# Sums of products in sixteen 32x32 tiles over four PSUM banks, block reads packed by parity, and one written-out order

## The reference, cut to what matters

```
a = k_l[..., :, None] * v_l[..., None, :]
out = einsum('bhs,bhst->bht', r_l, faaaa * a + s)
s = a + w_l[..., None] * s
```

## Time and profile before

| | us |
|---|---|
| three timed runs, median (lowest to highest) | 872.42 (869.52 to 874.44) |
| span of the profiled execution, first to last instruction | 871.9 |
| PE busy in it | 813.5 (93%) |
| DVE busy | 602.6 (69%) |
| ACT busy | 354.4 (41%) |
| POOL busy | 295.4 (34%) |
| PE share of the chain that ended last | 75% |

### The profile page before, as it was taken

One profiled execution on the slowest core, in us unless ns is written; L12 is line 12 of the kernel. 1 busy time (PEld: TensorE's weight loads), 2 busy tenths in 40 slices (PEclk: granted clock), 3 DMA queues, 4 the chain that ended last, 5 costly groups with the idle time before them and its releaser, 6 DMA issues.

```text
span 871.9 us, 18035 instructions
## 1 busy us (share of the span) xinstructions
PE 813.5 (93%) x7370; PEld 543.0 (62%) x7370; DVE 602.6 (69%) x1110; ACT 354.4 (41%) x715; POOL 295.4 (34%) x281
## 2 busy tenths in 40 slices
PE   6799999799989999899998999899998899999997
PEld 4577568457754676457773677546764377456674
DVE  1484966996589836996389945898369876893441
ACT  1322336524552427324454155524174156225422
POOL 2043741474028410474007620284104821640000
PEclk9899999999999999999999999999999899999999
DMA  9830103000010001100011001200002000100000
GB/s 300 327 97 1 49 2 123 1 2 2 26 49 2 1 26 49 49 1 2 26 49 50 1 3 51 71 1 2 2 2 73 0 3 2 49 1 3 25 25 24
DMA packets 17026, 34.20 MB, mean 39 GB/s; under 512 B 2224, under 2 KB 3888, under 8 KB 16944
## 3 DMA queue, kind: packets, MB, share of 16 engines
q1 hardware_dynamic: 14048, 31.20, 10.5%
q10 hardware_dynamic: 2896, 1.86, 0.7%
HBM read 24.66 MB, written 8.39 MB: 38 GB/s over the span
## 4 chain that ended last, share of the span: by engine, by line
PE 75%; DVE 12%; issue 6%; ACT 4%; POOL 2%; DMA 1%; DVEq 0%; ACTq 0%; POOLq 0%
PE PB L528 24%; PE PC L535 13%; PE CH L624 5%; PE PC L528 4%; PE CH L682 3%; DVE xmix L1565 3%; PE PC L717 3%; PE CH L661 3%; PE PB L379 3%; DVE av L1659 2%; PE PA L402 2%; PE PA L509 2%; PE PB L489 2%; PE CH L468 2%; POOL xmix L2057 1%
## 5 line engine op out<-in xcount | busy, mean ns | idle before, releaser
L2057 POOL TENSOR_TENSOR xmix<-xmix,xa 128x512 f32<-128x512 f32 x80 | 94.0, 1195 | 166.9 <-DVE xmix L1565 166.9
L2070 POOL TENSOR_TENSOR prod<-RA,K 128x512 f32<-128x512 f32 x112 | 127.2, 1161 | 23.7 <-DVE RA L1629 20.9
L1238 ACT ACTIVATE st<-av,half 32x512 f32<-32x512 f32 x64 | 74.7, 1167 | 44.5 <-DVE av L1712 43.1
L624 PE MATMUL CH<-prod,ones 32*32 32x512 f32 (+1 forms) x1152 | 75.8, 582 | 13.8 <-DVE av L1659 8.9
L1565 DVE SCALAR_TENSOR_TENSOR xmix<-PA,chan,sx 128x256 f32<-128x256 f32 x128 | 52.9, 475 | 39.0 <-PE PA L509 37.4
L1659 DVE TENSOR_TENSOR av<-CH,vT 128x512 f32<-128x512 f32 x112 | 71.7, 681 | 10.5 <-PE CH L624 10.3
L1670 DVE TENSOR_REDUCE yred<-av 128x64 f32<-128x512 f32 (+2 forms) x112 | 70.9, 674 | 0.0
L717 PE MATMUL PC<-sq_Wo,y 128*128 128x512 f32 x128 | 62.6, 621 | 6.8 <-DVE y L1755 6.8
L2082 POOL TENSOR_TENSOR K<-K,W 128x512 f32<-128x512 f32 x8 | 15.3, 1914 | 143.4 <-DVE prod L1595 143.4
L528 PE MATMUL PB<-xmix,sq_Wk 128*128 128x256 f32 x256 | 61.7, 386 | 0.0
L535 PE MATMUL PC<-sq_fWr,sxc 128*128 128x512 f32 x128 | 60.4, 612 | 0.0
(11 more groups left out here) (163 smaller groups left out, 1388.5 us busy)
## 6 DMA issues: line engine op xcount, KB each, us to landing
x<-x_rows SPq DMA_DIRECT2D x11, 512.0 KB, 3.4
x<-in_x SPq DMA_DIRECT2D x8, 512.0 KB, 3.9
x_rows<-x SPq DMA_DIRECT2D x8, 512.0 KB, 4.7
out_x<-x SPq DMA_DIRECT2D x8, 512.0 KB, 2.8
ctx_t<-in_ctx SPq DMA_DIRECT2D x5, 512.0 KB, 3.8
y<-in_ctx SPq DMA_DIRECT2D x3, 512.0 KB, 8.4
sq_Wk<-in_square SPq DMA_DIRECT2D x1, 1024.0 KB, 13.6
sq_Wv<-in_square SPq DMA_DIRECT2D x1, 1024.0 KB, 16.7
```

Of the source, the lines that this page charges most:

```text
L624: mm = pe.matmul(out, ones16[rows, rows], v, start=True, stop=True)
L1238: act.activation(st[p, :, :, 32 * q:32 * q + S], src, ACT.Copy, scale=half[p, 0:1]).then_inc(st_ready, 1)
L2057: pool.tensor_tensor(m, m, xa[:, ct:ct + 2, 1:L + 1], ALU.add).then_inc(mix_ready, 1)
L2070: pool.tensor_tensor(by_pair(prod[:, g % 4, :], h), r, k, ALU.mult).then_inc(prod_pool, 1)
```

## The change

It has four parts.

1. `CH` and `PA` become one tile `CHPA` of four banks. A visit now takes four slots of `prod`, one for each `ct` (quarter of the channels), into four banks: four row groups by four column groups, sixteen 32x32 tiles. A batch has five visits: diagonal with h = 1 (384 columns), h = 2 (256 columns), h = 4, and h = 8 twice (512 columns each). The products for a visit can be formed only when the visit before has read all of `prod`, and a visit shares two of its banks with the mixes and the turned rows, so the callers pass further waits (`*free`).
2. `st` has both halves of the batch at once, 64 columns per block: even blocks in rows 0 to 63, odd blocks in rows 64 to 127. r is kept in `RP` in the same packing, by four ACT instructions on 64 partitions after the last scaling of RA. The reads are again 32 products a half, on 64 moving columns in place of 128, and both halves follow one filling of eight ACT and eight DVE instructions.
3. `keep_warm` is called only at the start, no more for batch 7.
4. `fill`, `iteration` and `drain` are replaced on every engine by one written-out `program()` with another order in every batch. Values are turned by 32 per `ct` (the host rolls Wv to match; `ident` has 96 more columns).

```diff
-        Rz = sb("Rz", [P, 2 * (F + S)])
+        RP = sb("RP", [P, CT, 2, L])
-        st = sb("st", [P, CT, NB, P])
+        st = sb("st", [P, CT, 2, NSLOT // 2, P // 2])
-        PA = ps("PA", [P, 1024])
-        CH = ps("CH", [P, 1024])
+        CHPA = ps("CHPA", [P, 2048])
+        CH, PA = CHPA[:, 0:1024], CHPA[:, 1024:2048]
...
         # PE
-            def b_chunks(u, lo, hi):
...
-                    for q in range(4):
-                        for turn in range(2):
-                            rows, o = slice(32 * q, 32 * (q + 1)), 32 * ((q + turn) % 4)
...
-                            mm = pe.matmul(out, ones16[rows, rows], v, start=True, stop=True)
+            def b_visit(u, v, *free):
...
+                n = [L + P, L, CHUNK, CHUNK, CHUNK][v]
+                for q in range(4):
+                    rows = slice(32 * q, 32 * (q + 1))
+                    for ct in range(CT):
+                        o = 32 * ((q + ct) % 4)
+                        mm = pe.matmul(CHPA[o:o + 32, ct * CHUNK:ct * CHUNK + n], ones16[rows, rows], prod[rows, ct, 0:n],
+                                       start=True, stop=True)
+                        if q == 3:
+                            mm.then_inc(chunk_mm, 1)
...
             def b_reads(u, t):
-                    keep_warm(PB, 8)
...
-                            mm = pe.matmul(CH[32 * q:32 * (q + 1), t * C + ct * P:t * C + (ct + 1) * P],
-                                           R_OF_BLOCK[e][:, o:o + 32], st[:, ct, 2 * q + e, :],
+                            mm = pe.matmul(CH[32 * q:32 * (q + 1), o:o + P // 2],
+                                           RP[:, ct, hh, t * P + 32 * q:t * P + 32 * (q + 1)], st[:, ct, hh, 4 * t + q, :],
...
         # ACT
+                for e in range(2):
+                    for hh in range(2):
+                        src, dst = slice(64 * hh, 64 * (hh + 1)), slice(64 * e, 64 * (e + 1))
+                        act.activation(blocks_of(RP[dst, :, hh, :], e), blocks_of(cols(RA[src]), e), ACT.Copy).then_inc(R_kept, 1)
...
         # POOL
+            def b_prods(u, v):
+                h = VISITS[v]
+                pool.wait_ge(R_up, 4 * u + INTRA.index(h))
+                pool.wait_ge(K_up, 4 * u + INTRA.index(h))
+                pool.wait_ge(chunk_mm, N_VISITS * CT * u + CT * v)
...
         # PE, part of the new order (batch 3 in stage b)
+                a_first_mixes(4, (xa_ready, 25))
+                c_value(1, 0, 0)
+                b_visit(3, 0, (mix_scaled, 42))
+                c_receptance(1, 1, 1)
+                a_decay(4)
+                b_visit(3, 1)
+                c_value(1, 0, 1)
+                c_value(1, 1, 0)
+                c_value(1, 1, 1)
+                c_turn_y(2, 0)
+                a_decay2(4)
+                c_turn_y(2, 1)
+                b_visit(3, 2)
+                c_wo(2, 0, 0)
+                c_wo(2, 0, 1)
+                c_wo(2, 1, 0)
+                c_wo(2, 1, 1)
+                b_visit(3, 3)
+                a_key(4, 0)
+                a_key(4, 1)
+                c_turn(2, 0)
+                a_key(4, 2)
+                a_mix(4, 2, (av_ready, 68))
+                c_turn(2, 1)
+                a_key(4, 3)
+                b_visit(3, 4, (mix_scaled, 46))
```

More of the change, by code:

```diff
@@ L38, in build_xattn_rwkv @@
     SLOT_OF = {"w": 0, "k": 1, "v": 2, "r": 0, "g": 1}
[L41 to L47, removed]
+    VISITS = [1, 2, 4, 8, 8]
+    N_VISITS = len(VISITS)
+    N_WEIGHED = [2, CT, CT, CT, CT]
+    N_PRODS = [0, 2, CT, CT, CT]
+    N_RED = 2 + 3 * CT
     AHEAD = [1, 2, 3]
@@ L252, in wfactor @@
             return wblocks(h)[:, :, odd:odd + 1].to_broadcast([P, n, h])
[L254 to L260, removed]
-        def batch(i, lag):
-            return i - lag if 0 <= i - lag < B else None
-        def first(i, lag):
-            return i - lag if 0 <= i - lag < B and not ahead(i - lag) else None
         block = ctx.enter_context(nc.Block())
@@ L347, in fill @@
                 keep_x1(3)
-            def iteration(i):
-                b1, b4, b5 = (batch(i, n) for n in [1, 4, 5])
-                f1, f2 = (first(i, n) for n in [1, 2])
-                load_ctx(f1)
-                keep_x1(f2)
-                load_x(b1)
-                store(b5)
-                bring_x1(b4)
-            def drain():
+                load_x(2)
+                load_x(3)
+                bring_x1(0)
+                load_ctx(4)
+                load_x(4)
+                store(0)
+                bring_x1(1)
+                load_ctx(5)
+                keep_x1(4)
+                load_x(5)
+                store(1)
+                bring_x1(2)
+                load_ctx(6)
+                keep_x1(5)
+                load_x(6)
+                store(2)
+                bring_x1(3)
+                load_ctx(7)
+                keep_x1(6)
+                load_x(7)
+                store(3)
+                bring_x1(4)
                 store(4)
@@ L496, in a_ranks, with a_mix @@
                 mm.then_inc(rank_mm, 1)
-            def a_mix(a, step):
-                if a is None:
-                    return
-                pe.wait_ge(mix_scaled, 10 * a + (2 if step == 2 else 2 * step))
+            def a_mix(a, step, *free):
+                for f in free:
+                    pe.wait_ge(*f)
                 for ct in [0, 2, 1, 3]:
@@ L1048, in drain @@
                 c_value(7, 1, 1)
-            fill()
-            for i in range(3, 8):
-                iteration(i)
-            drain()
+            program()
         @block.scalar
@@ L2169, in _ @@
-            for i in range(5, 10):
-                iteration(i)
-            drain()
+            program()
 def kernel(**inputs):
```

1925 lines of the change are left out of this document (1216 added, 709 removed).

## The result

The changed kernel takes 851.1 us (median of four runs, 849.6 to 851.4), the kernel before 872.8 in the same comparison (869.5 to 874.4): a ratio of 0.974, 95% interval 0.972 to 0.976. Faster, by about 22 us; the forecast was 830, a gain of 42. The forecast's direction and its wide range (808 to 864) held; its own narrower range (815 to 848) did not.

A forecast was written before the change was run, and what follows sets the result against it. PE bounds the kernel, with DVE about as busy in the visit stage. 871.9 - 32.9 (sums) - 14.1 (reads) + 17 (waits) - 4 (start) - 8 (tail) = 829.9, predicted 830; own range 815 to 848, wide range 808 to 864.

The forecast's parts named there:

- Sums: Visits on PE: 10.5 us a batch becomes 5.85, saving 4.7 a batch, 32.9 us over seven batches.
- the bet on sixteen tiles: 512-column visits: sixteen tiles run in one turn, 1.10 us; rival of two turns, 1.9 us, total 856, chance 0.06.
- Reads: Reads on PE: 64 records in 1.0 us in place of 1.88, saving 1.76 us a batch, 14.1 in all.
- without that cover they would hold back the reads: ACT's four copies of r are hidden by PE's receptance and gate products; without these they would delay the reads.
- Added waits: PE waiting between visits, `prod` no longer double-buffered: +2.5 us in each of seven batches, +17, bounds 0 and +45.
- Start: Batch 0's statistics on DVE follow x1 directly, no longer behind an addition waiting for PE: -4 us, bounds 0 and -5.
- Tail: Batch 7's chain with real products in place of zeros -7, last fillings -1: -8 us, bounds +6 and -14.
- -1 for the fillings: Leaving out the tail's last four products of zeros: 4 us gained, +5 for lower clock, taken as -1.
- I take one and a half such cases over the tail's gaps, +5: Tail: half-clock stretches after PE idles, 3.4 us each, one and a half of them, +5 us.
- a rival (854): Low clock: longer waits between visits pull the clock down once a batch, 3.4 us x 7, 854; chance 0.09.
- my own sign of being wrong: The prediction is wrong if the granted clock falls in each batch; it was expected at 1.00 through the batches.
- DVE keeps the pace: Rival for the visit stage: the 32.9 us fall on time PE would wait anyway, 855; chance 0.16.

The follow-up runs named there:

- two-turn runs: Changed kernel with a visit's sixteen products on eight array tiles, output not the reference's: 863.1 us; with unused-result products in PE's waits as well: 858.4 us.
- restoring the clock: Changed kernel plus products with unused results, put into PE's waits inside the batches (second placing) and in the tail: 842.7 us, ratio 0.969.
- versions with fillings: Changed kernel plus unused-result products in PE's waits: first placing 860.5 us, second 843.1, tail alone 851.3, second and tail 842.7.
- fillings in the tail alone: Changed kernel plus 27 products with unused results, in the tail only: 851.3 us, ratio 0.977.
- last kernel: Changed kernel plus unused-result products in batches (fewer ahead of visit 1) and tail, h = 2 products in two halves, first half earlier on POOL: 851.9 us, ratio 0.977.

## Why the forecast was right in its sign and half the size

The forecast's terms, put on the same three stretches, and the spans:

| us gained | forecast | measured |
|---|---|---|
| up to the ranks of batch 2 | 4 + 6.5 - 2.5 = 8 | 4.9 |
| five periods | 5 x (6.5 - 2.5) = 20, and 13 moved out | 5.5 |
| rest | 8 + 4.7 + 3.5 - 2.5 = 14, less the 13 moved in | 12.5 |

The 13 us are seven groups of batch 4's stage c, which the new order leaves behind the ranks of batch 7 and the old one had ahead of them; the forecast did not speak of them, and they cancel in the sum. So the five periods gained 27 us less than the terms say, and start and tail together 9 more.

- *Sums, right in size.* A full visit is 1.07 us to the next start (475.78 to 476.85), forecast 1.10; the earlier trace rows carried the bet on sixteen tiles. What the saved time is worth is another question, below.
- *Reads, right.* 1.03 us for 64 records (541.23 to 542.26), forecast 1.0. But the gain hangs on the order: alone, in the order I gave it, part 2 costs 22 us. The sentence "without that cover they would hold back the reads" was the important one, and the price I had not put on it was 23.6 us of waits.
- *Added waits, too low.* Over the whole kernel the idle time is 83.4 against 88.6, but that is luck in the sum: in the five periods it grew by 18.1 us against 12.5, and the tail's fell short. For batches 1 to 5 I had about 10, 7 and three times 5 to 6 us; they are 11.2, 9.7, 5.4, 6.5 and 10.9. I had overlooked that batch 5 has visits 0 and 1 next to each other too, and had walked only batch 3's list between them, where the gap looked covered. Ahead of visit 1 PE waits for its four products on POOL, 0.81 us each: 3.75, 3.28, 0.93, 2.22 and 3.86 us in batches 1 to 5.
- *Start, luck.* Its term did come: the statistics of batch 0 begin at 23.09 us in place of 27.03, 3.9 earlier. But the new order puts half of layer 0 of batch 2 ahead of the first mixes, where it waits 6.42 us for its context from DMA, and these mixes start at 44.26 in place of 42.20, 2 us *later*. At the ranks of batch 1 one us is left of the four. The 4.9 us at the ranks of batch 2 hold batch 0's visits and reads, which the forecast counts apart.
- *Tail, better than forecast.* PE's idle time and fillings there fell by 16.8 us (39.8 to 23.0), where the terms come to 10.5 (8 and the 5 of the clock, less 2.5 of waits); at half level it has 13 us, as against 10. Also, my "-1 for the fillings" has the wrong sign: 4 us gained and 5 lost is +1, so the sum should have read 832.
- **The step that failed:** "I take one and a half such cases over the tail's gaps, +5", with "the granted clock at 1.00 through the batches". The tail was the wrong place and one and a half the wrong number: half-level time went from 24 to 78 us, in the five periods from 3 to 55, and PE's busy time grew by an estimated 20 us. In these periods busy time fell by 23.6 us in place of 45.3 (32.3, and the 13 moved out), so of the missing 27 us 22 are busy time and 6 are waits. I had this as a rival (854) and gave it 0.09, arguing that waits over 3 us lie in batch 1 only. In the batches it fell at or right after waits of 1.3 to 3.9 us; in the kernel before four single waits of 1.5 us, 102 us apart, left it at 1.00. That the clock falls in each batch was my own sign of being wrong, and it fell in each of the five periods.
- *DVE keeps the pace:* half true. The two-turn runs give 0.4 to 0.5 us a us of visit time, where the sum takes the 32.9 us of the visits in full. That the added waits, 17 us, stand for the other half is not shown. From visit 0 to visit 4 DVE is busy 27.5 of 34.6 us, 32.3 of 37.6, 30.8 of 32.8, 30.2 of 32.7 and 32.3 of 41.1 in batches 1 to 5 (forecast 30). So in batches 3 and 4 little is left but DVE's own time, in the others the waits and the clock are. The row of batch 3:

```profile
355.80:388.60 32.80, 30.45 (x241) 16.62 (x240) 30.82 (x52) 10.32 (x27) 26.33 (x27) 1.00 0.09 33
```

What stays open: restoring the clock brought PE's busy time to 745.5 but the timed median only to 842.7, 12 us above the forecast. With the clock restored the five periods are 15.5 us shorter than before, still 17 short of the terms: 7 of it is busy time, 10 are idle time and fillings. Fillings are not free, and single executions of the versions with fillings differ by 8 to 10 us, where the change's four differ by 2. How much of the 20 us lay on the path is bounded by 4 (ratios) and 13 (the two profiled spans), not settled. And parts 1 and 4, the sixteen tiles and the written-out order, were never run apart, so how the gain is shared between them is not shown.

## What to carry to other kernels

When a change shortens the busiest engine's work, ask what becomes of its clock: shorter bursts with the same waits between them leave it idle for a larger share, and here its busy time grew by an estimated 20 us that way. A shorter wait does not bring the clock back by itself: with 5.7 us less of it half-level time stayed as it was. A filling belongs at the start of a wait, in a bank that is free at that moment, and must end before it; one that ends 2 us late costs more than it saves. A part of a change that looks independent may lose alone, as the packed reads did. And compare forecast and trace stretch by stretch: here the sum of the idle time and the start looked right, and both were right by luck.

## What the runs showed of the hardware that I had not expected

- *PE stops inside dense bursts.* The block sums issue about 13 ns a record. The page of the last kernel lists a queue of kind "instruction":

```profile
q8 instruction: 59, 0.97, 0.5%
```

59 packets for 0.97 MB, 16 KB each, so the program seems to come in blocks. In the other kernels the block sums show no such stop, or one or two of 0.8 to 1.4 us; in the last one four, up to 3.8 us. That a block's end falls into a burst that uses instructions faster than they are brought would fit, and that other edits ahead of it shift the place; against it, the DMA engines moved next to nothing during three of the four (share 0.00). It was not tested and stays open. The Trainium skill ("Runtime: NRT & Kernel Launch", section "Instruction fetch mechanics") says that this loading is hidden, since instructions are issued more slowly than they come in. If the stops are this loading, these rows disagree; no run shows whether they are.

- *The clock's falls differ between versions that share their first 750 us.* With fillings in the tail alone (from about 760 us on) the ranks of batch 7 came at 656.7 in place of 652.3, with 62 us at half level in the five periods ahead of them in place of 55. What moves the falls was not found.
